# A fused eight-part network on one core: another order of token items and weight splits in the last stage

## The chip, the cores and the metric

One core of a Trainium2 chip. The metric is the device time of one execution in microseconds; the kernel before was run three times.

## The reference, cut to what matters

```python
x = x + L0_xattn(layernorm(x), ctx)      # 8 x 64 queries against 1601 context rows, 16 heads of 16
x = x + L0_attn(layernorm(x))
x = x + L0_ffn(layernorm(x))             # top-1 of 8 experts
x = x + L1_xattn(layernorm(x), ctx)
x = x + L1_attn(layernorm(x))            # scan s = s @ A.T + u, y = s @ C.T, gelu, norm
x = x + L1_ffn(layernorm(x))

# L1_ffn, on 512 tokens of 256:
def _moe_linear(x, router_w, expert_w):
    vals, idx = top_k(x @ router_w.T, 2)
    combine = einsum("tk,tke->te", softmax(vals), one_hot(idx))
    return sum(combine[:, e:e+1] * (x @ expert_w[e].T) for e in range(8))
g = _moe_linear(xt, router_gate, w_gate)       # 256 -> 1024
u = _moe_linear(xt, router_up, w_up)
d = _moe_linear(silu(g) * u, router_down, w_down)
```

## The kernel before, in words

The 512 tokens are four tiles of 128. Both cross attentions run as one loop of 16 rounds (layer and batch; `G` = 16), each of 13 steps `k` (`KT`). A step has the scores of 128 context rows (`S`), their exps on ScalarE (L1082), and the weighing of an earlier step (`W`, two behind). The other parts of the network hang on steps of the loop as named events, by hand-written tables: `SSM` is the second layer's scan and what follows it for one tile (`out`, `s_norm`, `s_turn`, `s_u`, `s_0` to `s_5`, `s_y`, `g_stats`, `g_norm`, `g_clean`, `m_stats`, `m_norm`, `m_turn`, `r_logits`, `r_pick`). "turn" is a transposition by TensorE (L848) and a copy by ScalarE; "stats" are statistics on DVE, after which GpSimd takes the root `rstd` (L604); "norm" is one DVE instruction (L1258). `r_logits` and `r_pick` give the router's weights `cmb`. For the last tile these events are in a list of their own, `TAIL`, worked off after the loop. Every engine walks the same lists in the same order, and each waits by semaphores for what it needs, so an instruction that waits holds up all behind it on its engine.

The experts of gate and up need the tokens scaled, transposed and split into a high and a low half precision part. That is a **token item**: `X` lists 40 of (gate or up, expert, first tile, last tile). Each is scaled by GpSimd (`scale_tokens`, L621, one instruction a tile, into one of two buffers `xg`), transposed by TensorE (`transpose_tokens`, L818) into one of two PSUM banks, copied by ScalarE (`xch`, L1110) and subtracted by DVE (`xcl`, L1346), after which the bank is free for the item two later. Items 0 to 7 stand at steps 2, 3, 4, 5, 6, 8, 9, 11 of the last round (`X_AT`), the others in `TAIL` as `x8` to `x39`. There `x` stands for all four engines' share of the item; GpSimd scales the item two ahead.

The weights come as 24 tiles of 1 MB through a ring of three `w32` by SyncE, which loads tile w when tile w - 3 has been split. A **weight split** is a ScalarE copy `wh` (L1097; `h2` in `TAIL`) and a DVE subtraction `wl` (L1338; `l2`), into a ring of four. Splits 0 and 1 stand at steps 7 and 10 of the last round (`SPLIT_AT`).

A `g` in `TAIL` is the next **gate part**: six matmuls of one expert, one gate unit, on tiles 0 and 1 (256 columns) or on tile 2 (128 columns), in the order of `GATE_PARTS`: 32 wide ones (units 0 to 3, eight experts each), then 32 narrow. They fill TensorE beside the events. A `d` is the same on tile 3, whose tokens come last; 32 of them close the stage. `O` and `out` finish the attention: `O` gives the sums, DVE divides, `out` multiplies with Wo, and DVE adds the result to `x` (L1388).

Then the rest of gate and up, and last the eight down experts: each writes four token tiles to PSUM, and DVE adds them to `x` (L1588) after all four. One DMA stores `x`.

## Time and profile before

| | us |
|---|---|
| median of 3 runs | 1051.88 |
| lowest and highest | 1049.47, 1052.98 |
| the profiled execution | 1051.81 |
| its span, first to last instruction | 1050.0 |
| TensorE busy | 955.4 (91%) |
| VectorE (DVE) busy | 630.1 (60%) |
| ScalarE (ACT) busy | 543.5 (52%) |
| GpSimd (POOL) busy | 214.6 (20%) |
| mean granted TensorE clock | 0.977 |

The busy times overlap: the engines work beside one another. A share of the span says nothing of where an engine waits, so the stretches are read one by one. The last round begins near 711 us, the tail at 749.8, the last `d` part ends near 827, the down experts run to 1045.

### The profile page before, as it was taken

What the parts mean: (1) busy time and instruction counts of PE and PEld (TensorE: products, weight loads), DVE (VectorE), ACT (ScalarE), POOL (GpSimd) and SP (SyncE); (2) the same over time, 40 slices, a digit from 0 to 9 for tenths busy, and PEclk for the clock granted to TensorE, in tenths of its full rate; (3) what the DMA queues carried; (4) which work ended last, traced back from release to release, by engine and by line L of the source; (5) the groups of instructions that cost most, each with busy time, mean ns of one, the idle gap of its engine ahead of it and who ended that gap; (6) DMA issues with size and microseconds to landing.
All of it is one profiled execution on the core that took longest, in us unless ns stands there. A gap on an engine that the chain in (4) does not pass through costs nothing.

```text
span 1050.0 us, 35583 instructions
## 1 busy us (share of the span) xinstructions
PE 955.4 (91%) x15476; PEld 630.7 (60%) x15476; DVE 630.1 (60%) x1047; ACT 543.5 (52%) x1020; POOL 214.6 (20%) x246
## 2 busy tenths in 40 slices
PE   5769889999999999999998898898798899999998
PEld 2446565656656666665665565566678544445887
DVE  5745756667485566757767667775653664445421
ACT  4558676676577676466555566567433321212200
POOL 4311112121111211112121121313348410000000
PEclk9989999999999999999999999999799999999999
DMA  8686376462734443454434434323311323232100
GB/s 276 172 285 208 90 214 160 142 178 71 207 93 155 107 121 79 117 124 117 116 100 110 107 101 116 80 66 133 112 50 41 121 83 118 81 105 96 41 1 21
DMA packets 70465, 123.78 MB, mean 118 GB/s; under 512 B 34420, under 2 KB 45716, under 8 KB 67048
## 3 DMA queue, kind: packets, MB, share of 16 engines
q1 hardware_dynamic: 69480, 119.84, 38.9%
q8 instruction: 124, 2.03, 0.8%
q0 software_dynamic: 544, 1.34, 0.4%
q10 hardware_dynamic: 288, 0.33, 0.1%
q14 instruction: 29, 0.24, 0.1%
HBM read 64.81 MB, written 17.31 MB: 78 GB/s over the span
## 4 chain that ended last, share of the span: by engine, by line
PE 66%; DVE 10%; issue 6%; ACT 6%; SPq 4%; DMA 4%; POOL 3%; ACTq 0%; POOLq 0%; DVEq 0%
PE ps L679 65%; SPq L445 4%; DVE mpart L1307 4%; POOL xg L621 3%; ACT p L1082 2%; DMA stage<-in_wkv 1%; DVE rinv L1324 1%; DMA c32b<-in_ctxT 1%; ACT ch L1040 1%; PE ps L818 1%; ACT k L1056 1%; ACT kh L1057 1%; PE ps L848 1%; DVE cl L1282 1%; DMA stage<-in_fw 1%
## 5 line engine op out<-in xcount | busy, mean ns | idle before, releaser
L1307 DVE TENSOR_REDUCE mpart<-ps 128x2 f32<-128x800 f32 (+1 forms) x256 | 252.6, 988 | 131.7 <-PE ps L679 130.8
L1082 ACT ACTIVATE p<-ps 128x512 f32<-128x512 f32 (+1 forms) x416 | 225.4, 595 | 187.7 <-PE ps L679 186.5
L609 POOL TENSOR_TENSOR kl<-k,kh 128x400 f16<-128x400 f32 (+1 forms) x128 | 117.5, 918 | 468.0 <-ACT kh L1057 468.0
L679 PE MATMUL ps<-p,v 128*17 128x64 f32 x6656 | 132.9, 224 | 0.0
L679 PEld LDWEIGHTS ps<-p,v 128*17 128x17 f32 x6656 | 99.5, 99 | 37.4 <-issue 35.5
L679 PE MATMUL ps<-wvh,ch 128*128 128x256 f16 (+1 forms) x416 | 115.1, 277 | 1.7 <-issue 1.7
L679 PE MATMUL ps<-wvh,cl 128*128 128x256 f16 (+1 forms) x416 | 114.3, 275 | 0.0
L679 PE MATMUL ps<-wvl,ch 128*128 128x256 f16 (+1 forms) x416 | 114.3, 275 | 0.0
L679 PE MATMUL ps<-xch,wh 128*128 128x512 f16 (+2 forms) x384 | 114.0, 311 | 0.0
L679 PE MATMUL ps<-xcl,wh 128*128 128x512 f16 (+2 forms) x384 | 113.9, 310 | 0.0
L679 PE MATMUL ps<-xch,wl 128*128 128x512 f16 (+2 forms) x384 | 113.8, 310 | 0.0
L679 PE MATMUL ps<-kh,qbcur 64*128 64x400 f16 (+1 forms) x512 | 87.0, 338 | 29.3 <-DVE mpart L1307 26.2
L679 PEld LDWEIGHTS ps<-qcur,ks 64*128 64x128 f16 (+1 forms) x3328 | 62.3, 97 | 73.1 <-issue 50.5
L1338 DVE SCALAR_TENSOR_TENSOR wl<-w,wh 128x2048 f16<-128x2048 f32 x24 | 55.2, 2302 | 84.6 <-ACT wh L1097 84.6
L679 PE MATMUL ps<-qcur,ks 64*128 64x64 f16 (+1 forms) x3328 | 86.9, 193 | 17.1 <-ACT p L1082 12.9
L679 PE MATMUL ps<-ch,wkh 128*128 128x400 f16 (+1 forms) x256 | 88.1, 344 | 6.7 <-ACT kh L1057 4.3
L679 PE MATMUL ps<-cl,wkh 128*128 128x400 f16 (+1 forms) x256 | 87.4, 341 | 0.0
L679 PE MATMUL ps<-ch,wkl 128*128 128x400 f16 (+1 forms) x256 | 87.4, 341 | 0.0
L1097 ACT ACTIVATE wh<-w 128x2048 f16<-128x2048 f32 x24 | 45.6, 1902 | 64.3 <-PE ps L679 64.1
L621 POOL TENSOR_SCALAR xg<-xm,cmb 128x256 f32<-128x256 f32 x64 | 63.4, 1006 | 47.7 <-PE ps L818 30.5
L679 PE MATMUL ps<-wh,ih 128*128 128x256 f16 x256 | 69.8, 273 | 0.0
L679 PE MATMUL ps<-wl,ih 128*128 128x256 f16 x256 | 69.8, 273 | 0.0
(203 smaller groups left out, 1482.3 us busy)
## 6 DMA issues: line engine op xcount, KB each, us to landing
ks<-kh SPq DMA_DIRECT2D x256, 100.1 KB
w<-in_wgu SPq DMA_DIRECT2D x16, 1024.0 KB, 4.8
ks<-kl SPq DMA_DIRECT2D x128, 100.1 KB
w<-in_wd SPq DMA_DIRECT2D x8, 1024.0 KB, 4.8
c32a<-in_ctxT SPq DMA_DIRECT2D x16, 400.5 KB, 5.2
cparts<-ch SPq DMA_DIRECT2D x8, 800.5 KB, 6.9
cparts<-cl SPq DMA_DIRECT2D x8, 800.5 KB, 9.3
c32a<-in_ctxT SPq DMA_DIRECT2D x12, 400.0 KB, 3.2
```

The source lines that it names most:

```text
L445: sp.dma_start(dst, src).then_inc(sem(name), 16)
L609: nc.gpsimd.tensor_tensor(kl[:, mt, k0:k0 + w], k32[:, ku % 2, 0:w], kh[:, mt, k0:k0 + w], ALU.subtract).then_inc(sem("klo_done"), 1)
L621: ins = nc.gpsimd.tensor_scalar(xg[:, i % 2, t - t0, :], xm[:, t, :], cmb[:, TT * r + t, e:e + 1], None, ALU.mult)
L679: return nc.tensor.matmul(o, lhsT, rhs, start=start, stop=stop, skip_group_check=shared)
L818: last = nc.tensor.transpose(o, xg[:, i % 2, t, P * kc:P * kc + P], ident[:, :])
L848: last = nc.tensor.transpose(mid[:, P * kc:P * kc + P], src[:, P * kc:P * kc + P], ident[:, :])
L1040: nc.scalar.activation(ch[u][:, kc, k0:k0 + w], c32[s][:, 0:w], ACT.Copy).then_inc(sem("chi_done"), 1)
L1056: nc.scalar.activation(k32[:, i % 2, 0:w], o[:, 0:w], func, **how).then_inc(sem("k32_done"), 1)
L1082: nc.scalar.activation(p32[0:n, step % PRING, BANK * side:BANK * side + BANK], ps[0:n, side, :], ACT.Exp, scale=DH ** -0.5).then_inc(sem(" ...
L1097: nc.scalar.activation(wh[:, w % W_RING, :], w32[:, w % 3, :], ACT.Copy, scale=W_SCALE)\
L1307: nc.vector.reduce_max(mpart[:, j0:j0 + 3:2, quarter], o.rearrange("p (b c) -> p b c", b=2)[:, :, 0:w], AX.X).then_inc(sem("max_done"), 1)
L1338: nc.vector.scalar_tensor_tensor(wl[:, w % W_RING, :], w32[:, w % 3, :], W_SCALE, wh[:, w % W_RING, :], ALU.mult, ALU.subtract).then_inc(s ...
```

## The change

Items 5 to 7 leave the loop for `TAIL`, and items 0 to 4 stand at steps 2, 4, 6, 9 and 12. Splits 0 and 1 stand one step later. Of the up items of tiles 0 and 1, two instead of four come before those of tile 3. `TAIL` has new places for nearly everything, and an item now has two entries there: `x` for GpSimd and TensorE, `y` for the copy and the subtraction. Gate parts of tile 2 come before units 2 and 3. From item 26 on, ScalarE scales the odd items (27 to 39), directly after its copy of the item two before; there are two semaphores `xg_ready0` and `xg_ready1` in place of one. A gelu of one column stands behind `s_u` of the last tile. The last down expert writes its four tiles to four banks, each tile is added when it is done, and stored by a DMA of its own; a `nop` and one wait go.

The two tables expand so around the places that matter (g and d with unit and expert left out):

```
before: g O x8 g g x9 g h2 l2 g out h3 x10 g g g g s_norm s_turn l3 g s_u ...
after:  x5 g O g x6 y5 g y6 g x7 g y7 h2 out x8 h3 g g g g g y8 s_norm s_turn l2 g s_u x9 ...
before: ... d d x28 h4 l4 d d x29 d d x30 d d x31 d d x32 h5 l5 ...
after:  ... d d x28 y28 h4 l4 d d x29 y29 d d x30 y30 d d x31 y31 d d x32 y32 h5 l5 ...
```

```diff
@@ -94,13 +94,14 @@
 POWERS_AT = {(0, 7): 0, (0, 9): 1, (0, 11): 2, (0, 12): 3, (1, 0): 4}
-SPLIT_AT = {(G - 1, 7): 0, (G - 1, 10): 1}
+SPLIT_AT = {(G - 1, 8): 0, (G - 1, 11): 1}
 
 
-X = [(0, e, 0, 2) for e in range(E)] + [(0, e, 2, 3) for e in range(E)] + [(1, e, 0, 2) for e in range(4)] + \
-    [(0, e, 3, 4) for e in range(E)] + [(1, e, 0, 2) for e in range(4, E)] + [(1, e, 2, 4) for e in range(E)]
-X_AT = {(G - 1, k): i for i, k in enumerate((2, 3, 4, 5, 6, 8, 9, 11))}
+X = [(0, e, 0, 2) for e in range(E)] + [(0, e, 2, 3) for e in range(E)] + [(1, e, 0, 2) for e in range(2)] + \
+    [(0, e, 3, 4) for e in range(E)] + [(1, e, 0, 2) for e in range(2, E)] + [(1, e, 2, 4) for e in range(E)]
+X_AT = {(G - 1, k): i for i, k in enumerate((2, 4, 6, 9, 12))}
 
-X_FIRST = {1: 0, 2: 8, 3: 20}
+X_SECOND, X_THIRD, X_BOTH = 8, 18, 26
 
 GATES = 4
-GATE_PARTS = [(n, e, 0, 2) for n in range(GATES) for e in range(E)] + [(n, e, 2, 3) for n in range(GATES) for e in range(E)]
+GATE_PARTS = [(n, e, *tiles) for units, tiles in (((0, 1), (0, 2)), ((0, 1), (2, 3)), ((2,), (0, 2)), ((2,), (2, 3)),
+                                                  ((3,), (0, 2)), ((3,), (2, 3))) for n in units for e in range(E)]
 LAST_GATE_PARTS = [(n, e, 3, 4) for n in range(GATES) for e in range(E)]
@@ -108,7 +109,8 @@
 
-TAIL = ("g O x8 g g x9 g h2 l2 g out h3 x10 g g g g s_norm s_turn l3 g s_u g s_0 x11 g s_1 x12 g s_2 x13 g s_3 x14 g "
-        "s_4 x15 g s_5 x16 s_y g g g g g_stats x17 g g g g_norm g_clean m_stats x18 g g g g m_norm m_turn g x19 r_logits "
-        "g g g g g g g r_pick").split()
+
+TAIL = ("x5 g O g x6 y5 g y6 g x7 g y7 h2 out x8 h3 g g g g g y8 s_norm s_turn l2 g s_u x9 g s_0 y9 x10 g s_1 y10 x11 g "
+        "s_2 y11 x12 g s_3 y12 x13 g s_4 y13 x14 g s_5 y14 x15 s_y y15 x16 g g g g g_stats y16 x17 g g g g g_norm "
+        "g g g g g_clean m_stats y17 g g g g g m_norm m_turn l3 g r_logits g g g g g g g g g g g r_pick").split()
 for e in range(E):
-    TAIL += ["g", "g", f"x{20 + e}"]
+    TAIL += ["g"] * min(2, len(GATE_PARTS) - TAIL.count("g")) + [f"x{X_THIRD + e}", f"y{X_THIRD + e}"]
 TAIL += ["g"] * (len(GATE_PARTS) - TAIL.count("g"))
@@ -116,4 +118,4 @@
     TAIL.append("d")
-    if n >= 7 and n % 2 and n < 31:
-        TAIL.append(f"x{28 + (n - 7) // 2}")
+    if n % 2 and 0 <= (n - 3) // 2 < len(X) - X_BOTH:
+        TAIL += [f"x{X_BOTH + (n - 3) // 2}", f"y{X_BOTH + (n - 3) // 2}"]
     if n % E == E - 1:
@@ -301,2 +303,3 @@
         half = sb(ctx, "half", [P, 1])
+        table = sb(ctx, "table", [P, 1])
         bT = sb(ctx, "bT", [P, KC, N])
@@ -425,3 +428,7 @@
 
-            return 6 + i % 2 if i < X_FIRST[2] else i % 2
+            return 6 + i % 2 if i < X_SECOND else i % 2
+
+        def scaled_by_act(i):
+
+            return X_BOTH <= i < len(X) and i % 2 == 1
 
@@ -435,2 +442,8 @@
 
+        def down_place(e, t):
+
+            if e == E - 1:
+                return ps[:, (6, 7, 2, 3)[t], 0:D]
+            return ps[:, 4 + 2 * (e % 2) + t // 2, D * (t % 2):D * (t % 2) + D]
+
         block = ctx.enter_context(nc.Block())
@@ -591,5 +604,6 @@
                 load(w32[:, w % 3, :], weight(w), f"w_in{w % 3}")
-            sp.wait_ge(sem("x_final"), 1)
-            load(out, x[:, :, :], "out_done")
-            sp.wait_ge(sem("out_done"), 16)
+            for t in range(TT):
+                sp.wait_ge(sem("x_final"), t + 1)
+                load(out[:, t, :], x[:, t, :], "out_done")
+            sp.wait_ge(sem("out_done"), 16 * TT)
 
@@ -622,11 +636,11 @@
                                                   ALU.mult)
-                ins.then_inc(sem("xg_ready"), 1)
+                ins.then_inc(sem(f"xg_ready{i % 2}"), 1)
 
             def event(name, layer, t):
-                if name == "r_pick" and t in X_FIRST:
+                if name == "r_pick" and t in (1, TT - 1):
                     for i in range(2):
-                        scale_tokens(X_FIRST[t] + i)
-                elif name == "x" and t + 2 < len(X) and t + 2 - X_FIRST[2] not in (0, 1) and \
-                        t + 2 - X_FIRST[3] not in (0, 1):
-                    scale_tokens(t + 2)
+                        scale_tokens((0 if t == 1 else X_THIRD) + i)
+                elif name == "x":
+                    if t + 2 < len(X) and t + 2 not in (X_THIRD, X_THIRD + 1) and not scaled_by_act(t + 2):
+                        scale_tokens(t + 2)
                 elif name == "q_stats":
@@ -810,5 +824,5 @@
                     pe.wait_ge(sem("row_done"), G)
-                elif i == X_FIRST[2]:
+                elif i == X_SECOND:
                     pe.wait_ge(sem("exp_done"), 2 * KT * G)
-                pe.wait_ge(sem("xg_ready"), i + 1)
+                pe.wait_ge(sem(f"xg_ready{i % 2}"), i // 2 + 1)
                 need(pe, "xcl_ready", i - 1)
@@ -1003,3 +1017,3 @@
                 for t in range(TT):
-                    o = ps[:, 4 + 2 * (e % 2) + t // 2, D * (t % 2):D * (t % 2) + D]
+                    o = down_place(e, t)
                     for it in range(IT):
@@ -1009,3 +1023,6 @@
                                       it == IT - 1 and n == 2)
-                last.then_inc(sem("d_mm"), 1)
+                    if e == E - 1:
+                        last.then_inc(sem("d_last"), 1)
+                if e < E - 1:
+                    last.then_inc(sem("d_mm"), 1)
 
@@ -1110,2 +1127,9 @@
                 nc.scalar.activation(xch[r][:, e, :, P * t0:P * t1], o, ACT.Copy).then_inc(sem("xch_ready"), 1)
+                if scaled_by_act(i + 2):
+                    r, e, t0, t1 = X[i + 2]
+                    act.wait_ge(sem("cmb_done"), t1)
+                    for t in range(t0, t1):
+                        ins = nc.scalar.activation(xg[:, i % 2, t - t0, :], xm[:, t, :], ACT.Copy,
+                                                   scale=cmb[:, TT * r + t, e:e + 1])
+                    ins.then_inc(sem(f"xg_ready{i % 2}"), 1)
 
@@ -1168,2 +1192,5 @@
                        .then_inc(sem("scan"), 1)
+                    if t == TT - 1:
+                        act.wait_ge(sem("half_ready"), 1)
+                        nc.scalar.activation(table[:, :], half[:, :], ACT.Gelu)
                 elif name == "s_y":
@@ -1549,4 +1576,6 @@
                         divide(G - 1, half)
-                elif item[0] in "xl":
-                    event("x" if item[0] == "x" else "w", 1, int(item[1:]))
+                elif item[0] in "yl":
+                    event("x" if item[0] == "y" else "w", 1, int(item[1:]))
+                elif item[0] == "x":
+                    continue
                 else:
@@ -1581,3 +1610,4 @@
             for e in range(E):
-                dve.wait_ge(sem("d_mm"), e + 1)
+                if e < E - 1:
+                    dve.wait_ge(sem("d_mm"), e + 1)
                 if e + W_RING < E:
@@ -1586,8 +1616,11 @@
                 for t in range(TT):
-                    o = ps[:, 4 + 2 * (e % 2) + t // 2, D * (t % 2):D * (t % 2) + D]
+                    if e == E - 1:
+                        dve.wait_ge(sem("d_last"), t + 1)
+                    o = down_place(e, t)
                     ins = nc.vector.scalar_tensor_tensor(x[:, t, :], o, cmb2[:, 2 * TT + t, e:e + 1], x[:, t, :],
                                                          ALU.mult, ALU.add)
-                ins.then_inc(sem("y_added"), 1)
-            dve.wait_ge(sem("y_added"), E)
-            nc.vector.nop().then_inc(sem("x_final"), 1)
+                    if e == E - 1:
+                        ins.then_inc(sem("x_final"), 1)
+                if e < E - 1:
+                    ins.then_inc(sem("y_added"), 1)
```

## Rows read from the trace of the kernel before

**Rows 1.** The page's row of granted TensorE clocks, 40 slices of 26.25 us each

```profile
PEclk9989999999999999999999999999799999999999
```

**Rows 2.** Windows: stretch, its length, each engine's busy us (instructions), granted clock, DMA

```profile
735.00:740.00 5.00, 1.74 (x18) 1.44 (x20) 3.26 (x3) 1.08 (x4) 4.33 (x3) 0.65 0.36 110
...
750.00:755.00 5.00, 5.00 (x40) 4.29 (x39) 3.65 (x8) 2.22 (x3) 3.21 (x4) 0.99 0.40 165
...
805.00:810.00 5.00, 2.77 (x28) 2.52 (x27) 3.49 (x3) 1.65 (x4) 5.00 (x4) 0.81 0.27 79
```

**Rows 3.** Timeline of PE, 738 to 789 us: start, duration, instruction, idle before it

```profile
738.26 0.66 PE L848 MATMUL ps<-ident,xm 128*128 128x128 f32 x2 [3.36 <-DVE xm L1258]
...
749.78 0.39 PE L679 MATMUL ps<-xch,wh 128*128 128x256 f16 x1
...
754.27 1.89 PE L679 MATMUL ps<-wo,oT 128*128 128x256 f32 x8
...
760.71 0.41 PE L848 MATMUL ps<-ident,xn 128*128 128x128 f32 x2 [1.71 <-DVE xn L1258]
...
781.52 0.41 PE L848 MATMUL ps<-ident,xm 128*128 128x128 f32 x2 [1.95 <-DVE xm L1258]
...
788.51 0.44 PE L818 MATMUL ps<-ident,xg 128*128 128x128 f32 x2 [0.83 <-POOL xg L621]
```

**Rows 4.** Chain that ended last, 740 to 900 us: start, duration, what

```profile
765.22 1.00 PE ps L679 x8
...
826.61 73.55 PE ps L679 x338
```

**Rows 5.** ACT: its timeline, 740 to 780 us, then one line of the groups

```profile
743.57 1.89 ACT L1097 ACTIVATE wh<-w 128x2048 f16<-128x2048 f32 x1
...
771.42 1.28 ACT L1171 ACT_TABLE_LOAD   x1
...
772.71 0.38 ACT L1171 ACTIVATE g_a<-ps 128x256 f32<-128x256 f32 x1
...
L1120 ACT ACTIVATE xh<-xnT 128x256 f16<-128x256 f32 x4 | 1.7, 417 | 0.1
```

**Rows 6.** Timeline of DVE, 734 to 776 us

```profile
734.81 2.28 DVE L1338 SCALAR_TENSOR_TENSOR wl<-w,wh 128x2048 f16<-128x2048 f32 x1
...
737.54 0.57 DVE L1258 TENSOR_SCALAR xm<-x,mv,rstd 128x256 f32<-128x256 f32 x1 [0.46 <-POOL rstd L604]
...
757.58 0.41 DVE L1388 TENSOR_TENSOR x<-x,ps 128x256 f32<-128x256 f32 x1
...
775.83 0.42 DVE L1258 TENSOR_SCALAR g_n<-g_a,mv,rstd 128x256 f32<-128x256 f32 x1
```

**Rows 7.** Timeline of POOL: the root (L604) before two of the norms

```profile
734.98 2.54 POOL L604 TENSOR_TENSOR rstd<-ve,half 128x1 f32<-128x1 f32 x1 [2.17 <-DVE ve L1253]
...
774.05 0.56 POOL L604 TENSOR_TENSOR rstd<-ve,half 128x1 f32<-128x1 f32 x1 [0.52 <-DVE ve L1253]
```

**Rows 8.** Stage of d parts: who waited 740 to 900 us, then timelines around 808

```profile
PE ps L818 <- POOL xg L621: 8.3, 7, 2.2
...
808.33 1.11 PE L818 MATMUL ps<-ident,xg 128*128 128x128 f32 x4 [2.23 <-POOL xg L621]
...
805.19 2.29 DVE L1338 SCALAR_TENSOR_TENSOR wl<-w,wh 128x2048 f16<-128x2048 f32 x1 [1.11 <-ACT wh L1097]
...
807.40 1.28 DVE L1346 TENSOR_TENSOR xcl<-ps,xch 128x512 f16<-128x512 f32 x2
...
805.59 2.68 POOL L621 TENSOR_SCALAR xg<-xm,cmb 128x256 f32<-128x256 f32 x1
```

**Rows 9.** The end: timeline of DVE; DMA issues (KB each, median us to landing)

```profile
1044.90 1.66 DVE L1588 SCALAR_TENSOR_TENSOR x<-ps,cmb,x 128x256 f32<-128x256 f32 x4 [8.82 <-PE ps L679]
...
out<-x SPq DMA_DIRECT2D x1, 512.0 KB, 2.9
...
qscratch<-qh SPq DMA_DIRECT2D x8, 64.0 KB, 1.8
```

## The prediction

> **What bounds the kernel now.** I read the page first. Its row of granted clocks has one dip, slice 29, 735 to 761 us, and that is the one place of the second half where TensorE is not nearly full [rows 1]. So the reader should go to 735 to 830 us, where the last round of the loop and the tail lie, and ask the windows there: from 735 to 740 us TensorE works 1.74 us of 5 and the mean granted clock falls to 0.65, and it is back at 0.99 from 750 on; from 805 to 810 us it works 2.77 us at 0.81 [rows 2]. The clock has two levels, 1.2 and 2.4 GHz; in both stretches the low one goes with a TensorE gap of over 2 us. Then the timeline of PE, for the gaps themselves. They are 3.36 us before the transposes called m_turn at 738.26, 1.71 before s_turn, 1.95 before the last m_turn, 0.83 before item 20 [rows 3], and 2.23 before item 31; this last pattern comes three times (items 31, 35, 39), and all seven waits for GpSimd's scaled tokens make 8.3 us [rows 8]. From 826.61 the chain of waits is TensorE alone, 73.55 us in one piece [rows 4]. TensorE's work is the same before and after, so the change is worth what it takes out of these gaps, out of the low clock, and out of the last 5 us.
>
> **The last round, up to the first gate part (749.78).** m_turn waits for m_norm on DVE (737.54), which waits for the root on GpSimd. That root took 2.54 us where the same instruction takes 0.56 at 774.05 [rows 6, 7]: it began 0.17 us after the 2.28 us subtraction of weight split 0 and ended 0.4 us after that. The change puts split 0 one step later, behind m_norm. That takes 1.98 us off. Items 1 and 2 move from steps 3 and 4 to 4 and 6, items 3 and 4 to 9 and 12; so two DVE subtractions (0.64 each by the pair of 1.28) [rows 8] leave the stretch between the gelu and m_norm: 1.3 us. The gelu at its start stays where it is. Together m_turn goes from 738.26 to about 735.0 to 735.2.
>
> Behind it stand r_logits, three exp pairs and split 1. Before, ScalarE did split 1 (1.89 us at 743.57) ahead of step 11's exps [rows 5]; after, behind them and ahead of step 12's. The sum of ScalarE work until the last exps is the same less one item's copy of 512 columns (0.5 to 0.6, where 256 columns take 0.42 [rows 5]), so the loop ends near 745.8, 4.0 us sooner. The bounds: 1.5 (only the 1.98 us of the root, less some new wait) to 5. The new wait would be for the l half of split 1: 2.3 us on DVE now directly before item 4's subtraction and the copy of the sums, which gives about 746.8 for that copy; the tail reaches its first use near 747, so I count nothing for it, 0 to 1 if it is late.
>
> Three items, 5 to 7, are now done in the tail. An item of two tiles takes TensorE about 0.44 us (x31 to x32 shows the same at half clock, 1.11 [rows 8]): plus 1.3. TensorE still waits some 2.4 us for m_turn, over the 2.23 that stands beside a low clock and the 1.95 that doesn't (the slice of 781 us in the row of clocks shows a 9) [rows 1, 3, 8]. I take it that the clock falls again and that some 1 us of dense work of the tail runs at half speed: plus 0.5, bounds 0 and 2.
>
> **The tail, up to item 28.** Two chains run beside the filler: O, divide, out, layer norm, s_turn; and s_y, gelu, norm, clean, norm, m_turn.
> First chain: split 2's subtraction (2.3 us on DVE) stood before the sum of `out`, which began 757.58 [rows 6] although its matmuls, 1.89 us from 754.27, ended 756.2 [rows 3]. It moves behind s_turn: 1.4 us less. Against that, subtractions 5, 6 and 7 (1.9 us) now stand between divide and `out`, and item 7 can't be transposed before subtraction 5 is done, which follows two divides (2.5 us): a new TensorE gap of about 0.8. The five gate parts before s_turn (five by 0.65) then cover the rest, so the 1.71 us gap [rows 3] goes.
> Second chain: from the end of s_y's matmuls, where the table load begins (771.42), to m_turn (781.52) it is 10.1 us [rows 3, 5]. The gelu waited for a table load of 1.28 us [rows 5]; it is loaded behind s_u now. Only 0.5 of this shows, since subtraction 15 stands before the statistics. The norm at 775.83 came 1.2 us after the root (774.05 plus 0.56), behind item 17's subtraction [rows 6, 7]; item 16's transposes now follow s_y at once and its subtraction lies under the root. So 8.5 us. The work laid beside it is 15 parts of 0.335, 2 of 0.655 and two items, 7.2 us (a large part takes 1.00 with its scan step, of which the scan's two matmuls are a third [rows 4]; a small one is half as wide). Gap 1.3 instead of 1.95.
> The table load in its new place stands before item 9's copy on ScalarE. From there to item 11, which needs item 9, TensorE has some 2.5 us of work and the load, copy and subtraction take 2.4: I count 0. It must also survive until the gelu: the copies between don't reload it, as the gelu's own table served them before, and the next load stands first at the exp of the router.
> Third: split 3's subtraction now follows m_norm on DVE (2.3 us), in front of r_logits, which is ready 2.1 us after it: nothing. From m_turn to item 20 was 6.99 us with 0.83 idle [rows 3]; now 7.4 us of gate parts stand there: this gap goes.
> In sum the gaps 1.71 + 1.95 + 0.83 = 4.49 become 0.8 + 1.3 = 2.1: minus 2.4, bounds 0 and minus 4.5. With the round: -4.0 + 1.3 + 0.5 - 2.4 = -4.6. Dating each step instead gives 797.2 for the end of item 28, which was 802.56: -5.4. I take -5.0.
>
> The Trainium skill, "ScalarE: Activation LUTs", section "What ACT_TABLE_LOAD costs", puts a drain of about 1.38 us on top of the load of 1.28. Here the load ended 772.70 and the gelu began 772.71 [rows 5], behind an engine that was already idle, so no row bears the drain out. By the page item 9's copy would come 1.4 us later and leave a gap of about 1 us before item 11; the time would be 1 us more, 1044.8.
>
> **The stage of d parts.** The chain of waits names GpSimd's scaling, and the change gives the odd items from 27 on to ScalarE, so one expects much. I don't, and this is the choice on which the forecast rests most. Item 31 waited until 808.33. GpSimd's scaling of it, stretched to 2.68 us beside the subtraction of weight split 4 (805.19, 2.29 us), ended 808.27. But the subtraction of item 29, which frees the bank of item 31, stands behind the same split on DVE and ended about 808.05 (two items from 807.40 in 1.28 us) [rows 8]. Items 35 and 39 show the same pattern. The order of copies, splits and subtractions in this stage is unchanged, so 0.2 us of each 2.2 goes, and of the short waits for GpSimd (8.3 less 0.83 and three by some 2.1, about 1.1) a third to a half: about 1.0. ScalarE's scaling isn't in the trace; the nearest row is a 128x256 activation out of SBUF, 0.42 us [rows 5], so 0.8 for an item, 6 us for seven, under TensorE's work as long as it doesn't hold up a split. Bounds: the two stretches at half clock after items 31 and 35 vanish (1.1 each) with the waits: -3.5; each of three splits comes half a us late: +1.5. I take -1.0.
>
> **Between 827 and 1044.** Nothing changes: weights 5 to 7 are loaded later, but the buffer of weight 6 is free after split 3 near 778 and needed near 820.
>
> **The end.** The last expert's four additions (1.66 us from 1044.90) [rows 9] become one behind the last matmul, 0.41: minus 1.25. The store of 512 KB took 2.9 us to land; now the last is 128 KB, between that and the stores of 64 KB (1.8) [rows 9]. It is nearer to the small one; I take 2.1: minus 0.8, bounds 0 and -1.1. Term: -2.05.
>
> **Sum.** -5.0 - 1.0 - 2.05 = -8.05 us. On the profiled execution, 1051.81 us with a span of 1050.0, that is 1043.8; the median of the runs, 1051.88, is 0.07 above that execution, so the same figure holds: 1043.8.
>
> **Rivals.**
> A, as summed: 1043.8, own range 1041.5 to 1046.5. Chance 0.52.
> B, the low clock goes too. The gaps end up just under those that were followed by it (2.23 against the 1.95 that wasn't) [rows 3, 8]. Then what TensorE does between m_turn and the router's result, some 4 us at half clock, is 1.9 shorter, the 0.5 goes, and the d stage yields 2 more: 1039.4. For it: every gap named gets shorter. Against: 2.4 remains before m_turn. 0.19.
> C, new waits in the place of the old ones: ScalarE's scaling and split 1 ahead of the last exps, the late item 7. The loop yields 2 instead of 4 and the d stage costs 1.5 instead of giving 1: 1043.8 + 2 + 2.5 = 1048.3. For it: ScalarE and DVE work in one order written by hand, and an item 0.5 us late moves a split of 1.9 and 2.3 us. 0.19.
> D, the change doesn't do what it says: the placement moves waits but removes none, only the end stays: 1049.8. 0.06. Against: the stretched root is a collision of two known instructions.
> E, slower. The clock that falls before m_turn stays low into the tail. Low time was about 736.5 to 750 before (1.5 us at full and 3.5 at half give the 0.65 [rows 2]), four times the gap that it came with. Each us of dense work at the low level loses half; from 745.8 the tail is dense. The gain of 8.05 is gone after 16 us of it, near 762; if it lasted to m_turn near 776 it would cost 15: 1059. Against: before, the clock was back as soon as the dense gate parts began at 749.78 [rows 2, 3]. 0.04.
>
> **How the numbers follow.** Likeliest is A: 1043.8. B to C spans 1039.4 to 1048.3; with the edges of their bounds 1039.5 to 1049.0, which leaves out E, most of D and a little below B. A change of 0.3%, 3.2 us, is about what a measurement of this kernel can tell from none: the limit is 1048.7. Faster: A, B and just over half of C, 0.82. Same: the rest of C, and D: 0.13. Slower: E and a little: 0.05.
>
> **What would show it.** The root before the first m_turn at 0.56 us and m_turn near 735; the first gate part near 746; a gap of about 0.8 before item 7; s_y to the last m_turn 8.5 us; item 28 near 797; gaps of some 2 us still before items 31, 35 and 39, ended by DVE; one table load behind s_u and none before the gelu; the last addition 0.4 us and the last store about 2 us. Wrong if these gaps before 31, 35 and 39 are gone (then GpSimd was the bound, 4 to 6 us more), or if ScalarE's scaling takes far over 0.5 us a tile.

## The result, and the profile after

The changed kernel takes 1040.68 us (median of 4 runs, 1040.10 to 1040.78) where the kernel before takes 1050.68 in the same comparison; the ratio is 0.9903, interval 0.9885 to 0.9921. A second comparison gave 1039.89 and 0.989 (0.9859 to 0.9921). So the gain is 10.0 us in the first and 11.7 in the second, forecast were 8.05; the time forecast was 1043.8, the range 1039.5 to 1049.0.

The page of the changed kernel, span, TensorE, ScalarE, GpSimd and granted clock. The dip of [rows 1] stands in the same slice, 8 tenths in the place of 7:

```profile
span 1039.0 us, 35578 instructions
...
PE 950.1 (91%) x15476; PEld 627.0 (60%) x15476; DVE 628.6 (61%) x1047; ACT 549.3 (53%) x1035; POOL 200.6 (19%) x232
...
PEclk9989999999999999999999999999899999999999
```

Windows of the changed kernel (stretch, its length, busy us and instructions of PE, PEld, DVE, ACT and POOL, granted clock, DMA share, GB/s). They answer to [rows 2]: the low level (1.2 GHz of 2.4) now lasts from about 739.2 to 746.0 instead of 736.5 to 750 (0.8 us of the first window, all of the second, 1.0 of the third), and between 805 and 810 it is gone. It stands between 810 and 815 instead:

```profile
735.00:740.00 5.00, 3.24 (x120) 2.60 (x118) 4.51 (x18) 3.59 (x8) 2.73 (x2) 0.92 0.47 161
...
740.00:745.00 5.00, 5.00 (x114) 4.15 (x110) 3.47 (x5) 2.87 (x4) 2.26 (x2) 0.50 0.22 70
745.00:750.00 5.00, 4.14 (x32) 3.25 (x30) 3.17 (x6) 1.19 (x2) 3.07 (x4) 0.90 0.52 197
...
805.00:810.00 5.00, 2.44 (x33) 2.11 (x31) 3.89 (x4) 3.41 (x5) 4.12 (x4) 1.00 0.14 51
...
810.00:815.00 5.00, 5.00 (x51) 4.86 (x49) 2.19 (x4) 4.46 (x7) 2.49 (x3) 0.66 0.59 210
```

TensorE's timeline of the changed kernel (start, duration, instruction, idle time before it and what ended it), the places of [rows 3, 8]. The first line is the marker used below, the eight row transposes at the start of the last round:

```profile
708.46 0.61 PE L693 MATMUL ps<-ident,m 128*1 128x128 f16 x8 [1.04 <-DVE m L1343]
...
734.52 0.41 PE L862 MATMUL ps<-ident,xm 128*128 128x128 f32 x2 [1.69 <-DVE xm L1285]
...
739.57 0.66 PE L693 MATMUL ps<-qcur,ks 64*65 64x64 f16 x16 [1.56 <-ACT p L1099]
...
749.98 0.63 PE L832 MATMUL ps<-ident,xg 128*128 128x128 f32 x4 [0.86 <-DVE xcl L1373]
...
756.32 0.38 PE L862 MATMUL ps<-ident,xn 128*128 128x128 f32 x2
...
767.17 0.66 PE L832 MATMUL ps<-ident,xg 128*128 128x128 f32 x4 [0.46 <-POOL xg L635]
...
775.15 0.41 PE L862 MATMUL ps<-ident,xm 128*128 128x128 f32 x2 [0.53 <-DVE xm L1285]
...
802.31 0.63 PE L832 MATMUL ps<-ident,xg 128*128 128x128 f32 x4 [2.13 <-DVE xcl L1373]
...
809.72 0.63 PE L832 MATMUL ps<-ident,xg 128*128 128x128 f32 x4 [2.29 <-DVE xcl L1373]
...
817.40 0.63 PE L832 MATMUL ps<-ident,xg 128*128 128x128 f32 x4 [1.40 <-DVE xcl L1373]
```

The gap before m_turn went from 3.36 to 1.69 us, that before s_turn is gone, that before the last m_turn went from 1.95 to 0.53. The 0.83 before the first item of tile 3 is gone too. Two are new, 0.86 before item 7 (749.98) and 0.46 before item 16 (767.17). The three before items 31, 35 and 39 are still there, and DVE's subtraction ends them now.

The end, DVE and the DMA issues (KB each, us to landing), answering to [rows 9]:

```profile
1036.32 0.48 DVE L1620 SCALAR_TENSOR_TENSOR x<-ps,cmb,x 128x256 f32<-128x256 f32 x1 [2.14 <-PE ps L693]
...
out<-x SPq DMA_DIRECT2D x4, 128.0 KB, 1.7
```

**How the traces are compared.** The long loop ahead of the last round ends at a different time in each trace: the marker stands between 705.56 and 710.46 us, for kernels whose instructions ahead of it are the same. That is as much as the parts of this change are worth. So every place below is counted from the marker of its own trace (before: 708.78), in us; the first three are the starts of TensorE's transposes or matmuls of that name. The median times of the runs hold this scatter, the places don't:

| trace | m_turn | O | last m_turn | last d part ends | last matmul ends | span ends |
|---|---|---|---|---|---|---|
| before | 29.48 | 41.93 | 72.74 | 118.34 | 336.10 | 341.22 |
| changed | 26.06 | 37.66 | 66.69 | 110.07 | 327.84 | 330.54 |
| a_again | 26.06 | 36.26 | 65.46 | 109.95 | 327.71 | 330.33 |
| b_split | 27.43 | 38.86 | 70.99 | 117.89 | 336.71 | 341.80 |
| u_split | 28.05 | 41.43 | 70.45 | 114.74 | 334.19 | 336.84 |
| b_scale | 29.40 | 41.84 | 72.67 | 116.90 | 334.66 | 339.81 |
| u_scale | 26.11 | 36.31 | 65.54 | 112.71 | 330.47 | 333.10 |
| u_table | 26.07 | 37.63 | 66.93 | 110.59 | 328.35 | 331.00 |
| u_l2 | 26.07 | 36.26 | 67.58 | 111.88 | 330.23 | 332.85 |
| u_last | 26.42 | 37.89 | 66.92 | 110.39 | 328.15 | 333.23 |
| m_late | 26.16 | 37.57 | 66.74 | 106.53 | 324.29 | 326.98 |
| m_late2 | 26.07 | 36.26 | 65.47 | 105.56 | 323.32 | 325.94 |
| m_share | 26.07 | 37.60 | 65.98 | 104.43 | 322.19 | 324.83 |
| m_share2 | 26.43 | 36.64 | 65.18 | 105.27 | 323.03 | 325.67 |

Of the 10.7 us between the first two lines 3.4 come before m_turn, 0.85 between it and O, 1.8 between O and the last m_turn, 2.2 between that and the last d part, nothing in the 217.8 us of dense matmuls, 2.4 behind the last matmul. Between two places the kernels don't do the same work: the change has moved items and gate parts across them. So only the undos below say what a part is worth.

### The profile page after: what moved, and what is told of

The parts are those of the page before. It is cut to its first block, busy times and chain, and to the rows that moved or that the text cites. A ratio compares the mean times of both kernels' runs of the same rounds, so it can differ in the third digit from the quotient of the medians.

```text
span 1039.0 us, 35578 instructions
## 1 busy us (share of the span) xinstructions
PE 950.1 (91%) x15476; PEld 627.0 (60%) x15476; DVE 628.6 (61%) x1047; ACT 549.3 (53%) x1035; POOL 200.6 (19%) x232
## 4 chain that ended last, share of the span: by engine, by line
PE 69%; DVE 13%; ACT 8%; issue 5%; DMA 3%; SPq 1%; POOL 1%; ACTq 0%; DVEq 0%; POOLq 0%
PE ps L693 67%; DVE mpart L1334 4%; ACT p L1099 3%; DVE rinv L1351 1%; SPq L458 1%; DMA stage<-in_wkv 1%; ACT ch L1057 1%; DMA c32b<-in_ctxT 1%; PE ps L832 1%; DVE cl L1309 1%; ACT kh L1074 1%; ACT k L1073 1%; DVE wl L1365 1%; PE ps L862 1%; DMA stage<-in_fw 1%
## 5 line engine op out<-in xcount | busy, mean ns | idle before, releaser
L693 PE MATMUL ps<-qcur,ks 64*128 64x64 f16 (+1 forms) x3328 | 86.1, 192 | 18.4 <-ACT p L1099 15.2
L693 PE MATMUL ps<-wh,il 128*128 128x256 f16 x256 | 69.8, 273 | 0.0
```

The costliest lines, as they stand in the source:

```text
L693: return nc.tensor.matmul(o, lhsT, rhs, start=start, stop=stop, skip_group_check=shared)
```

## Experiments

### The splits of the last round: one part undone, and one part alone

Undone in the changed kernel (u_split):

```diff
-SPLIT_AT = {(G - 1, 8): 0, (G - 1, 11): 1}
+SPLIT_AT = {(G - 1, 7): 0, (G - 1, 10): 1}
```

> The changed kernel with weight splits 0 and 1 back at steps 7 and 10 of the last round. Theory 1, the root before m_norm is held up by split 0's DVE subtraction: the root takes 2.5 us again instead of 0.56, m_turn comes about 2.0 us later than 734.5, the clock falls before it and the low stretch is 13 us instead of 7, the first gate part comes about 4 us later: 1044 to 1045. Rival, the fewer items in the loop are what brought the first gate part forward, by 0.6 us of ScalarE and DVE each, and the place of the splits gives nothing: 1040.7 to 1041.2.

Measured 1044.23 us (1043.45 to 1046.35), ratio to before 0.9943 (0.9924 to 0.9961): 3.6 us more than the changed kernel. GpSimd's root and two of TensorE's waits in u_split:

```profile
730.47 2.54 POOL L618 TENSOR_TENSOR rstd<-ve,half 128x1 f32<-128x1 f32 x1 [2.83 <-DVE ve L1280]
...
733.61 0.66 PE L862 MATMUL ps<-ident,xm 128*128 128x128 f32 x2 [2.54 <-DVE xm L1285]
...
741.83 0.66 PE L693 MATMUL ps<-qcur,ks 64*65 64x64 f16 x16 [2.70 <-ACT p L1099]
```

The root takes 2.54 us again, m_turn comes 1.99 us later, and O 3.8 us later. Theory 1 holds in each of its places. Counted from the marker, the last matmul ends 6.3 us later and not 3.6. Of this 1.7 us lie in the dense matmuls behind the stage of d parts (219.5 us where the changed kernel takes 217.8): there the clock was low in this trace for a while. The rest of m_turn's gain, 1.4 us (28.05 against 29.48 before), is left with the splits back in their old place; it goes with the items, for which 1.3 was forecast.

The same line alone in the kernel before (b_split):

> The kernel before with weight splits 0 and 1 one step later (steps 8 and 11) and nothing else. Theory 1: the root before m_norm takes 0.56 us, m_turn comes at 736.3 instead of 738.26, the first gate part 2 us or more sooner than 749.78 (more if the clock stays up), time 1048 to 1050 where before takes 1051. Rival: item 5 at step 8 and the items at every step use up what the root gives, m_turn moves by under 0.5 us, time as before.

One run, 1051.64 us: no gain. The root and m_turn behave as expected, m_turn 2.05 us sooner:

```profile
734.12 0.56 POOL L604 TENSOR_TENSOR rstd<-ve,half 128x1 f32<-128x1 f32 x1 [2.17 <-DVE ve L1253]
...
735.43 0.41 PE L848 MATMUL ps<-ident,xm 128*128 128x128 f32 x2 [2.44 <-DVE xm L1258]
```

At the last m_turn 1.75 us of it is left, at the last d part 0.45, and behind it the clock was low for a while, in dense matmuls that cost 1.06 us more than before's. So neither sentence is right on the time: the mechanism is there, and in this one execution, with its low clock elsewhere, nothing of it reaches the end. At m_turn the split's new place yields the same in both orders, 2.05 and 1.99 us. At O it yields 3.1 us in the old order and 3.8 or 5.2 in the new (against the changed kernel's two traces); how long the clock stayed low differs between these traces as well, so what the order adds isn't shown.

### Who scales the items: undone, and alone

u_scale, undone:

```diff
         def scaled_by_act(i):
 
-            return X_BOTH <= i < len(X) and i % 2 == 1
+            return False
```

> The changed kernel with all items scaled by GpSimd again (nothing on ScalarE). Theory 1, the DVE order is the bound and GpSimd's scaling is only 0.2 us behind it: the gaps before items 31, 35, 39 are 0.2 us longer, three short waits come back, and the low clock may follow the longer gaps as before: stage of d parts 22.9 to 24.6 us instead of 21.9, time 1041.7 to 1043.3. Rival, GpSimd was the bound and ScalarE's help is what gives the gain of the stage: gaps before nearly every item, 4 to 6 us more, 1044.7 to 1046.7.

Measured 1043.61 us (1041.44 to 1045.89), ratio 0.994 (0.9919 to 0.996): 2.9 us more, and by the places of the traces 2.6 to 2.8. The intervals of the two ratios just touch. From the last m_turn to the last d part it takes 47.17 us, the changed kernel 43.38 and 44.49. TensorE in u_scale:

```profile
793.30 0.65 PE L832 MATMUL ps<-ident,xg 128*128 128x128 f32 x4 [0.48 <-POOL xg L635]
...
795.11 0.66 PE L832 MATMUL ps<-ident,xg 128*128 128x128 f32 x4 [0.48 <-POOL xg L635]
...
796.91 0.65 PE L832 MATMUL ps<-ident,xg 128*128 128x128 f32 x4 [0.48 <-POOL xg L635]
...
800.46 1.11 PE L832 MATMUL ps<-ident,xg 128*128 128x128 f32 x4 [2.23 <-POOL xg L635]
```

Items follow one another at 1.81 us, which is GpSimd's two instructions of 0.9, where TensorE needs 1.11. Between long gaps GpSimd is the bound here, which neither the recorded prediction nor theory 1 had; the long gaps are 2.06 and 2.23 us as before, which the rival had not. The result lies between the two. The old order is no different in this. In b_split, where the clock was up behind item 34, items follow one another at 1.80 us as well:

```profile
818.76 0.66 PE L818 MATMUL ps<-ident,xg 128*128 128x128 f32 x4 [0.47 <-POOL xg L621]
...
820.56 0.66 PE L818 MATMUL ps<-ident,xg 128*128 128x128 f32 x4 [0.48 <-POOL xg L621]
```

b_scale, alone in the kernel before (odd items from 29 on, two semaphores as in the change):

> The kernel before with one part of the change: ScalarE scales the odd items from 29 on. Theory 1, the long gaps before items 31, 35 and 39 are made by the order split, subtraction, item on DVE: they stay at about 2.0 us each and are now ended by DVE's subtraction; only the waits of 0.3 to 0.5 us for GpSimd go, and with them part of the low clock; the stage from the end of item 28 to the last d part takes 22 to 23.5 us instead of 24.6, time 1 to 2.6 us less than before: about 1048.5 to 1049.5. Rival, GpSimd's scaling was the bound there: the long gaps go, the stage takes about 18.5 us, time near 1044.5.

Measured 1049.72 us (10 runs, 1047.11 to 1054.04), ratio 0.9987 (0.9971 to 1.0002). From item 28's start to the last d part it takes 23.6 us, before 25.0. TensorE in b_scale:

```profile
804.14 0.66 PE L822 MATMUL ps<-ident,xg 128*128 128x128 f32 x4 [0.27 <-POOL xg L625]
...
807.59 1.09 PE L822 MATMUL ps<-ident,xg 128*128 128x128 f32 x4 [2.12 <-DVE xcl L1357]
...
816.25 0.63 PE L822 MATMUL ps<-ident,xg 128*128 128x128 f32 x4 [2.13 <-DVE xcl L1357]
...
823.95 0.63 PE L822 MATMUL ps<-ident,xg 128*128 128x128 f32 x4 [1.43 <-DVE xcl L1357]
```

This is the step of the prediction as it was written: with half the scaling gone from GpSimd the long gap before item 31 is 2.12 instead of 2.23 us, and the name at its end changes from GpSimd to DVE. The two had stood 0.2 us apart. The rival falls. The last gap, 1.43 instead of 2.05, is shorter also because items 36 and 37 ran at the low clock here, so that TensorE came later. GpSimd's row of the kernel before says how near the two bounds were: it scaled items 30 to 39 without a pause,

```profile
802.89 23.00 POOL L621 TENSOR_SCALAR xg<-xm,cmb 128x256 f32<-128x256 f32 x20 [4.54 <-PE ps L818]
```

which is 2.3 us an item of two tiles. Relieving it gains 1.4 us in this trace, and then the order on DVE holds.

### What bounds the stage of d parts: the splits taken out of it

m_late, on the changed kernel:

```diff
-    if n % E == E - 1:
-        TAIL += [f"h{GATES + n // E}", f"l{GATES + n // E}"]
+    if n == E - 1:
+        TAIL += ["h4", "l4"]
+TAIL += ["h5", "l5", "h6", "l6", "h7", "l7"]
```

> The changed kernel with weight splits 5 to 7 (ScalarE copy and DVE subtraction) moved from inside the stage of d parts to behind it; split 4 stays. Theory 1, the splits that stand in front of an item's copy and subtraction on ScalarE and DVE bound this stage: the gap before item 31 (2.1 us) stays, those before items 35 and 39 (2.3 and 1.4 us) go, the clock doesn't fall there, items come in pairs 2.7 us apart, the stage from the end of item 28 to the last d part takes 17.2 us instead of 21.9, time about 1036.0. Rival, the scaling is the bound: the gaps stay whatever the splits do, 1040.7. Second rival, TensorE then waits for split 5 in front of the second unit after the stage: up to 4 us of the gain comes back, 1038 to 1040.

Measured 1035.94 us (1034.69 to 1036.57), ratio 0.9861 (0.9845 to 0.9878). Split 7 stood behind the last d part before already, so it is splits 5 and 6 that leave the stage. TensorE in m_late, items 31, 36 and 38:

```profile
799.82 0.63 PE L833 MATMUL ps<-ident,xg 128*128 128x128 f32 x4 [2.13 <-DVE xcl L1374]
...
807.46 0.66 PE L833 MATMUL ps<-ident,xg 128*128 128x128 f32 x4 [0.27 <-POOL xg L636]
...
810.17 0.66 PE L833 MATMUL ps<-ident,xg 128*128 128x128 f32 x4 [0.27 <-POOL xg L636]
```

One gap of 2.13 us stays, at the split that stayed; the other two, before items 35 and 39, are gone, the pairs are 2.71 us apart, and behind the stage TensorE has no wait that the changed kernel doesn't have. Both rivals fall. The stage is 18.4 us from item 28's end, not 17.2, because the clock was low behind the gap that is left. A second comparison:

> The kernel with splits 5 to 7 behind the stage of d parts again, beside the next one on the same chip: 1035.9 plus or minus 1, 4 to 5.5 us under the changed kernel.

1036.8 us (1034.7 to 1038.53), ratio 0.9843 (0.9814 to 0.9873), beside 1039.89 for the changed kernel: 3.1 us there. Against the changed kernel's own first comparison m_late's 1035.94 is 4.7 us less. The places from the last m_turn to the last d part, 39.8 and 40.1 against 43.4 and 44.5, say 3.6 and 4.4 in these pairs.

### A version on top of it

m_share is m_late with these two edits:

```diff
-            return X_BOTH <= i < len(X) and i % 2 == 1
+            return X_BOTH <= i < len(X) and i % 3 != 2
...
-TAIL = ("x5 g O g x6 y5 g y6 g x7 g y7 h2 out x8 ...
+TAIL = ("x5 g O g x6 y5 g y6 g g x7 y7 h2 out x8 ...
```

> The kernel with splits 5 to 7 behind the stage of d parts, and two changes more: ScalarE scales two of three items from 27 on instead of every other, and item 7 stands one gate part later. Theory: what paces the stage of d parts once the splits are out of it is GpSimd's cycle of 2.7 us for a pair (two scalings of 0.92, the transposes and the waits between); with a third of the items on GpSimd the pace is TensorE's own 1.11 us an item, so the stage loses the waits of 0.27 us and ends about 1.5 us sooner, one gap of 2.1 us (split 4) stays; item 7's gap goes from 0.9 to about 0.3. Time about 1034.0. Rival, ScalarE becomes the bound with 1.3 us an item (copy 0.5, scaling 0.8): no change against 1035.9, or 1 us more.

1034.47 us (1033.05 to 1037.04), ratio 0.9832 (0.9814 to 0.9851), and once more beside m_late2:

> The kernel with splits 5 to 7 behind the stage and two of three items scaled by ScalarE again: 1034.5 plus or minus 1, 1 to 2 us under the one before it. Rival: the two are the same, within 0.5 us.

1035.5 us (1033.67 to 1036.95), ratio 0.9832 (0.9809 to 0.9855). Both times its median is 1.3 to 1.5 us under m_late's, with intervals that overlap, so that it is faster than m_late isn't shown; it has the lowest medians here, 17.0 and 16.1 us under the kernel before (1051.45 and 1051.55 in these comparisons). The gap before item 7 is 0.21 us, as expected. The stage itself gained less than expected, for its remaining long gap grew:

```profile
803.81 0.63 PE L833 MATMUL ps<-ident,xg 128*128 128x128 f32 x4 [2.93 <-DVE xcl L1374]
```

That is 2.93 us in the place of 2.13. ScalarE's timeline of m_share says why:

```profile
798.04 0.90 ACT L1133 ACTIVATE xg<-xm,cmb 128x256 f32<-128x256 f32 x2
798.84 1.90 ACT L1115 ACTIVATE wh<-w 128x2048 f16<-128x2048 f32 x1
```

With two of three items on ScalarE, item 30 is scaled there, directly ahead of the copy of split 4. The copy, the split's subtraction and item 29's subtraction behind it come about 0.8 us later, and item 31 waits for the last of them. In m_late the copy of the split follows item 28's copy at once. So the rival, ScalarE as the bound, is true at this one place.

### The table load, split 2, the last expert, and the same kernel again

u_table takes the gelu of one column and its wait out of `s_u`.

> The changed kernel without the gelu of one column behind s_u. The table load of 1.28 us returns between s_y's matmuls and the gelu. The blind sum gave the early load 0.5 us, since subtraction 15 stood between; the changed kernel's trace shows that subtraction over before the gelu ends, so by it the last m_turn comes 1.2 us later, counted from s_y, and the gap before it is 1.7 instead of 0.5 us. Rival, the load was hidden anyway: no change.

1040.14 us in one run. From O to the last m_turn 29.30 us, in the changed kernel 29.03 and 29.20: at most 0.3 us. ScalarE and GpSimd in u_table, then GpSimd in the changed kernel:

```profile
765.33 1.28 ACT L1195 ACT_TABLE_LOAD   x1
...
764.10 3.63 POOL L635 TENSOR_SCALAR xg<-xm,cmb 128x256 f32<-128x256 f32 x4 [0.41 <-PE ps L832]
...
767.96 0.56 POOL L618 TENSOR_TENSOR rstd<-ve,half 128x1 f32<-128x1 f32 x1 [0.23 <-DVE ve L1277]
```

```profile
765.29 3.63 POOL L635 TENSOR_SCALAR xg<-xm,cmb 128x256 f32<-128x256 f32 x4 [0.40 <-PE ps L832]
...
768.88 0.56 POOL L618 TENSOR_TENSOR rstd<-ve,half 128x1 f32<-128x1 f32 x1
```

In the changed kernel the gelu is 1.1 us sooner, counted from s_y, and the root that needs its statistics stands on GpSimd behind the scaling of items 16 and 17, which ends at 768.9. Without the early load the statistics come 0.2 us after GpSimd is done. Neither the 0.5 of the recorded sum nor the 1.2 expected here is there; the rival is nearly right, for a reason that it didn't name.

u_l2 puts `l2` back: `y7 h2 l2 out` and `s_turn g s_u`.

> The changed kernel with split 2's DVE subtraction back ahead of the sum of out. Theory: that sum begins 2.3 us later (behind ScalarE's copy of split 2 and the subtraction), s_turn likewise, with a TensorE gap of about 2.2 us before it. Rival: the gate parts before s_turn hide it and s_turn moves by under 0.5 us.

1044.35 us in one run. The transposes of s_turn in u_l2:

```profile
758.38 0.41 PE L862 MATMUL ps<-ident,xn 128*128 128x128 f32 x2 [1.93 <-DVE xn L1285]
```

From item 7 to s_turn 8.43 us, in the changed kernel 6.34 (756.32 less 749.98): 2.1 us, a gap of 1.93, and it is still there at the last m_turn (31.3 us from O instead of 29.0). The theory holds, and the 1.4 of the prediction was low.

u_last puts the last expert and the store back as they were.

> The changed kernel with the last expert as before: four additions after all four tiles, one store of 512 KB. Both theories of the rest leave this alone: from the last matmul to the end of the span 5.1 us instead of 2.7, time 2.4 us more than the changed kernel, 1043. Rival, the smaller stores cost as much as they hide: less than 1 us.

1041.85 us in one run. From the last matmul to the end of the span 5.08 us, in the changed kernel 2.70: 2.4 us as expected. The time of the one run is 1.2 us over the changed kernel's first median and 2.0 over its second, which stood beside it.

a_again is the changed kernel itself.

> The changed kernel once more, unchanged, for a second trace. Theory: the same instructions with the same gaps of 2.1 us are followed by the low clock in one execution and not in another, so places move by 1.2 us in the last round (item 7's transposes 40.3 or 41.5 us after the last round's eight row transposes) and by 1 us for each gap in the stage of d parts; time 1040.7 plus or minus 1.5. Rival, the clock is decided by the program: every place as in the first trace within 0.2 us.

1039.89 us (1039.13 to 1043.86). Two windows of a_again, to be held against the same stretches above, and item 31:

```profile
740.00:745.00 5.00, 5.00 (x95) 4.11 (x89) 3.89 (x4) 2.38 (x5) 3.35 (x3) 0.82 0.27 74
...
800.00:805.00 5.00, 5.00 (x48) 4.75 (x48) 1.81 (x3) 3.16 (x5) 2.55 (x4) 0.68 0.59 210
...
799.97 1.09 PE L832 MATMUL ps<-ident,xg 128*128 128x128 f32 x4 [2.13 <-DVE xcl L1373]
```

m_turn stands at 26.06 in both traces, O at 37.66 and 36.26; and behind the same gap of 2.13 us item 31's transposes take 1.09 us here and 0.63 there. The low clock of the last round lasted 6.8 us there and 3.4 here (granted clock 0.84 from 735 to 740 us, 0.82 from 740 to 745). So the low clock isn't decided by the program alone.

## Why the prediction was right, point by point

**The last round.** Forecast: the root 2.0 us less, m_turn 3.2 sooner, the loop's end 4.0. Measured: 2.0, 3.4, and 4.3 to 5.7 at O, by how long the clock stayed low. u_split shows the mechanism, and that the other 1.4 us of m_turn's 3.4 come with the items. The gap before m_turn was 1.69 us where 2.4 was expected, and the clock did not fall there, as I had taken it to. From 734.52 on TensorE still ran at the high level; the clock fell at about 739.2, in the gap of 1.56 us that ends at 739.57, before the last scores. Of the ten traces with this order and these splits only that of m_late has it fall right behind the gap before m_turn. That split 1 and item 4 would not hold up O by more than TensorE's own work is borne out in the changed kernel's two traces, where part of that work ran at the low clock. It isn't at the high clock: in u_scale, whose last round has the same instructions and no low clock between 730 and 750 us, TensorE waits for DVE's copy of the sums,

```profile
742.81 0.67 PE L693 MATMUL ps<-osum,sel 128*128 128x256 f32 x2 [0.42 <-DVE osum L1361]
```

and O comes at 36.31, where a_again with 3.4 us of low clock has it at 36.26. So a shorter low stretch than a_again's would have given nothing more at O.

**The tail.** Forecast: gap of 0.8 before item 7, none before s_turn, 1.3 before the last m_turn, 8.5 us from s_y to it, none before the first item of tile 3. Measured: 0.86, none, 0.53 and 0.46 (before item 16, which the sum didn't have), 8.44 (the matmuls of s_y, 0.70 from 766.01, to 775.15), none. Item 28 began 5.7 us sooner; I had taken 5.0 between 4.6 and 5.4. Inside it two terms are off in opposite directions: split 2 gave 2.1 and not 1.4, the early table load 0.3 at most and not 0.5. For that load I had written down GpSimd's scaling nowhere, though the same engine holds the root. The Trainium skill, "ScalarE: Activation LUTs", section "What ACT_TABLE_LOAD costs", has a drain of about 1.38 us on top of a load of about 1.28, by which the time would have been 1 us more. The load of 1.28 is in this trace, the drain isn't. ScalarE's timeline of the changed kernel:

```profile
758.27 1.28 ACT L1195 ACT_TABLE_LOAD   x1
...
759.56 0.20 ACT L1195 ACTIVATE table<-half 128x1 f32<-128x1 f32 x1
```

The load ended at 759.55 and the next activation began 0.01 us later.

**The stage of d parts.** Forecast: -1.0, the long gaps stay and DVE ends them. They stayed, and DVE ends them; b_scale and m_late show why. This is the term of the sum that was mis-sized: it gave 2.6 us in the first trace and 1.5 in the second (22.4 and 23.5 us from item 28's start to the last d part, before 25.0). TensorE's idle time in that stretch was 7.5 us before, 6.4 in the first trace and 5.9 in the second. So the waits gave 1.1 and 1.6 where 1.0 was forecast. The other 1.5 us of the first trace are the clock: before and in a_again it was low twice in the stage, in the first trace once, each time for 3.4 us by the granted clock. That was luck, and the sum had no term for it. What I had not seen is that GpSimd, at 1.8 us an item, is the bound between the gaps as soon as the clock is up (u_scale and b_split). Undoing ScalarE's help costs 2.9 us in the new order (u_scale), giving it yields 1.4 to 1.7 in the old (b_scale, an interval that touches zero). I can't say from these traces how much of that difference is the order and how much the clock.

**The end.** -2.05 forecast, -2.4 measured: the addition 0.48 us where 0.41 was taken; the stores of 128 KB took 1.7 us to land (median of the four) and not 2.1, no more than the 64 KB store of before (1.8).

**The rivals.** B (the low clock goes too) came half true: the time, 1040.7, lies between A and B, and the low clock of the last round shrank from 13.7 us to 6.8 and 3.4 but didn't go. C, new waits in the place of the old ones, is refuted where it was named: ScalarE's scaling takes 0.45 us a tile, half of this row of the changed kernel, beside the 0.42 of the nearest row, and in the changed kernel it holds up no split by more than some 0.2 us (split 5's copy, by the copy ahead of it that began 0.2 us after its transposes had ended). In m_share, with more of the scaling on ScalarE, it did hold one up, by 0.8:

```profile
795.74 0.90 ACT L1132 ACTIVATE xg<-xm,cmb 128x256 f32<-128x256 f32 x2
```

D falls by the time alone, and u_split, u_l2, u_scale and u_last each give back 2.3 us or more by the ends of the spans. Those four and u_table come to 14.3 us together, more than the 10.7 gained, since the low clock differs between the traces; they are not to be added up. The moves of items 5 to 7 and of two up items and the order of the gate parts were not undone alone, so their share isn't shown. E didn't come: in the eleven traces of this tail's order the low clock of the last round lasted at most 2.0 us into the tail.

## What to carry to other kernels

When two engines' waits end within 0.2 us of each other, the profile names only the later. Helping that one gains the 0.2; read from the code what else the waiting instruction needs, and date that too. Long work that isn't needed yet (here weight splits of 1.9 and 2.3 us, needed 10 us and more later) belongs behind a stage in which every engine passes short items on, not among them: that was worth 3 to 5 us, as much as the best part of the change. And an undo in the new order and an addition in the old order didn't give the same number here; where the traces also differ in their low clock, such a pair doesn't tell whether the order or the clock made the difference, and a place close behind the edit (m_turn, 1.99 and 2.05 us) tells more than the end of the span.

## What the runs showed of the hardware

**A clock that falls by chance.** Behind a TensorE gap of 2.12 to 2.13 us before item 31 the granted clock fell at once in a_again, b_scale and m_late2, and not in the changed kernel's first trace, in u_table or in u_last. In the last round, the same instructions had the low level for 6.8 us in the first trace and 3.4 us in a_again, and not at all between 730 and 750 in u_scale; the gap in which it fell was 1.56 us. One fall costs 1.1 to 1.7 us here: O comes 1.4 us later in the first trace than in a_again, and the dense matmuls behind the stage take 1.06 us more in b_split and 1.7 in u_split. The Trainium skill, "TensorE: Matmul & The Clock Gate", section "Part 1: The HAM clock gate", says of the slow matmuls at a kernel's start that the chip's watch runs free of the program and their number differs from run to run; these traces show such a difference in the middle of a kernel. A forecast of a few us on such a kernel can't be better than one or two such falls.

**An engine that stands still beside DVE.** GpSimd's instruction on one column took 2.54 us beside DVE's 2.28 us subtraction of two operands in SBUF, and 0.56 elsewhere; moving the subtraction restored it (u_split against the changed kernel, b_split against the kernel before). The Trainium skill, "SBUF — State Buffer", section "SBUF: two separate sides", describes a port pair that is an exclusive lock: a DVE operation with two inputs in SBUF and a GpSimd operation that reads SBUF can't both have it, and the second to start is blocked for the whole of the other. The runs agree: the root started 0.17 us after the subtraction and ended 0.4 us after it [rows 6, 7].
